# State-space stage of a transformer-like block: the residual as one more TensorE product of the output projection, rows copied out of PSUM by ScalarE

## What is computed

```python
def step(state, inp):                       # state [B, 512, 16]
    x_t, dt_t, B_t, C_t = inp
    dA = exp(clip(dt_t[:, :, None] * A[None], -10, 10))
    dB = dt_t[:, :, None] * B_t[:, None, :]
    state = clip(state * dA + x_t[:, :, None] * dB, -10, 10)
    y_t = einsum('bdn,bn->bd', state, C_t) + D * x_t
    return state, y_t
_, ys = lax.scan(step, state0, (x_in, dt, Bm, Cm))
y = ys * silu(z)
attn = y @ W_out                            # [.., 512] @ [512, 256]
x = x + attn + ffn(xn)                      # ffn: attention, shared expert, 2 of 7 routed experts
```

## Time and profile before

| | |
|---|---|
| median of 3 runs | 4429.94 us (4425.78 to 4437.9) |
| the profiled execution | 4428.19 us |
| its span, first to last instruction | 4426.1 us |
| mean granted TensorE clock | 0.930 of full speed |
| busy, whole span | TensorE 85%, VectorE 67%, ScalarE 57%, GpSimd 50% |
| addition of the residual, VectorE L1747 | 32 times, 682 ns each, at 2331.4 to 4422.8 us |

### The profile page before, as it was taken

One profiled execution on the slowest core, in us unless ns is written; L12 is line 12 of the kernel. 1 busy time (PEld: TensorE's weight loads), 2 busy tenths in 40 slices (PEclk: granted clock), 3 DMA queues, 4 the chain that ended last, 5 costly groups with the idle time before them and its releaser, 6 DMA issues.

```text
span 4426.1 us, 71771 instructions
## 1 busy us (share of the span) xinstructions
PE 3749.4 (85%) x22840; PEld 2837.4 (64%) x22840; DVE 2973.9 (67%) x5485; ACT 2502.8 (57%) x6473; POOL 2202.3 (50%) x1120
## 2 busy tenths in 40 slices
PE   4888888888888875999879888889998898888886
PEld 2444444444444434777658888878887888788776
DVE  4454444554545422222269999999999999999997
ACT  1443344334444341333278777788787787777773
POOL 2223333333333321000067777777777777777774
PEclk8899899999999987999989999999999999999998
DMA  2322232222322214666522222222222222222221
GB/s 85 96 82 83 79 95 82 84 79 93 97 88 85 81 51 117 212 213 208 161 89 92 76 87 78 80 87 87 75 92 85 78 92 76 87 80 78 87 82 36
DMA packets 285739, 419.89 MB, mean 95 GB/s; under 512 B 77397, under 2 KB 249814, under 8 KB 262808
## 3 DMA queue, kind: packets, MB, share of 16 engines
q1 hardware_dynamic: 273048, 381.12, 26.5%
q0 software_dynamic: 12288, 33.57, 2.2%
HBM read 330.63 MB, written 83.17 MB: 93 GB/s over the span
## 4 chain that ended last, share of the span: by engine, by line
POOL 22%; issue 10%; DVE 9%; PE 8%; ACT 1%; DVEq 0%; POOLq 0%; DMA 0%; SPq 0%; ACTq 0%
POOL m_ub L1516 18%; PE m_Y L1870 7%; DVE m_PR L1720 2%; DVE m_S L1728 2%; DVE m_PR L1728 2%; DVE m_S L1720 2%; POOL m_th_z L1501 1%; POOL m_yg L1526 1%; DVE m_ub L1705 1%; POOL m_dtx L1495 1%; ACT m_dA L1626 0%; PE m_F L1881 0%; PE m_F L1832 0%; PE m_F L1806 0%; DVEq L1719 0%
## 5 line engine op out<-in xcount | busy, mean ns | idle before, releaser
L1516 POOL TENSOR_TENSOR m_ub<-m_Bb,m_dtx 128x2048 f32<-128x2048 f32 x256 | 1157.5, 4544 | 436.3 <-PE m_Y L1870 429.9
L1626 ACT ACTIVATE m_dA<-m_dt,m_a_neg 128x128 f32<-128x128 f32 x4096 | 1211.1, 388 | 168.1 <-DVE m_S L1728 166.9
L1870 PE MATMUL m_Y<-m_ub,m_ident 128*128 128x128 f32 x8192 | 1040.9, 293 | 204.4 <-DVE m_ub L1705 204.4
L1870 PEld LDWEIGHTS m_Y<-m_ub,m_ident 128*128 128x128 f32 x8192 | 1022.7, 208 | 218.2 <-DVE m_ub L1705 218.2
L539 ACT ACTIVATE f_pt<-f_X 128x512 f32<-128x512 f32 (+1 forms) x704 | 372.2, 554 | 725.2 <-PE f_X L831 674.8
L615 DVE TENSOR_REDUCE f_nm<-f_Y 128x1 f32<-128x512 f32 (+3 forms) x896 | 434.1, 531 | 365.7 <-PE f_Y L825 339.6
L1720 DVE SCALAR_TENSOR_TENSOR m_PR<-m_dA,m_S 128x512 f32<-128x512 f32 x512 | 355.8, 695 | 123.1 <-POOL m_ub L1516 52.2
L824 PE MATMUL f_Y<-f_kst,f_qst 96*128 96x512 bf16 (+3 forms) x1024 | 281.9, 331 | 107.1 <-DVE f_nm L615 89.9
L1720 DVE SCALAR_TENSOR_TENSOR m_S<-m_dA,m_PR 128x512 f32<-128x512 f32 x512 | 355.1, 694 | 12.1
L1728 DVE CUSTOM_DVE_ANT_1 m_PR<-m_PR,m_ub 128x512 f32<-128x512 f32 x512 | 353.8, 691 | 0.2 <-DVE m_PR L1720 0.2
L1728 DVE CUSTOM_DVE_ANT_1 m_S<-m_S,m_ub 128x512 f32<-128x512 f32 x512 | 353.8, 691 | 0.0
(11 more groups left out here) (229 smaller groups left out, 6530.7 us busy)
## 6 DMA issues: line engine op xcount, KB each, us to landing
m_Bb<-m_bc_dram SPq DMA_DIRECT2D x64, 1024.0 KB, 4.5
m_Cb<-m_bc_dram SPq DMA_DIRECT2D x64, 1024.0 KB, 4.6
f_parts_dram<-f_parts SPq DMA_DIRECT2D x32, 768.0 KB, 4.1
f_kst<-f_parts_dram SPq DMA_DIRECT2D x192, 128.0 KB, 2.6
f_qst<-f_parts_dram SPq DMA_DIRECT2D x192, 128.0 KB, 2.6
e_rows<-sorted_rows SPq DMA_DIRECT2D x70, 256.0 KB, 2.7
e_wg<-Wg SPq DMA_DIRECT2D x70, 256.0 KB, 2.9
e_wu<-Wu SPq DMA_DIRECT2D x70, 256.0 KB, 3.9
```

The source lines that it names most:

```text
L1516: pool.tensor_tensor(ub[:, h, i, :, :], Bb[:, s, :, :], dtx[:, par, m, None, s * SN:(s + 1) * SN].to_broadcast([P, NST, SN]), ALU.mult).th ...
L1626: last = act.activation(dA[:, h, i, n, :], dtt[:, par, m, s * SN:(s + 1) * SN], ACT.Exp, scale=a_neg[:, m, n:n + 1])
L1870: last = pe.matmul(Y[:, i * SN:(i + 1) * SN], ident[:, :], ub[:, h, i, n, :], start=False, stop=(n == NST - 1), skip_group_check=True)
```

## The change

The addition leaves VectorE. In `project_out` each row block gets a seventh product, the identity times `res`, in the same accumulation, so `F[2]` holds the finished rows; TensorE now waits for `res_loaded`. ScalarE copies `F[2]` into `ot` (`copy_out`), behind `decays(c, par, 2)` and ahead of `softplus(c + 1)`, and signals `ot_done` as VectorE did.

```diff
@@ ScalarE @@
+        def copy_out(c):
+            act.wait_ge(outp_done, c + 1)
+            act.wait_ge(ot_stored, 16 * c)
+            act.activation(ot[:, :, :], F[2][:, :, :], ACT.Copy).then_inc(ot_done, 1)
...
             if not first:
                 decays(c, par, 2)
+                copy_out(c - 1)
...
-        chunk_order(body, lambda c, par: None)(nc.scalar)
+        def tail(c, par):
+            copy_out(c)
+        chunk_order(body, tail)(nc.scalar)
@@ VectorE @@
-        def add_res(c):
-            dve.wait_ge(outp_done, c + 1)
-            dve.wait_ge(res_loaded, 16 * (c + 1))
-            dve.wait_ge(ot_stored, 16 * c)
-            dve.tensor_tensor(ot[:, :, :], F[2][:, :, :], res[:, :, :], ALU.add).then_inc(ot_done, 1)
...
-                slots[1][1] = lambda: add_res(c - 1)
...
             gate_y(c, par, NU - 1)
-            add_res(c)
@@ TensorE, project_out @@
             pe.wait_ge(wdiag_ready, NY * (c + 1))
+            pe.wait_ge(res_loaded, 16 * (c + 1))
             pe.wait_ge(ot_done, c)
...
                 for k in range(TOPK):
-                    last = pe.matmul(F[2][:, j, :], wdiag[:, k, j, :], yg[:, k, j, :],
-                                     start=False, stop=(k == TOPK - 1))
+                    pe.matmul(F[2][:, j, :], wdiag[:, k, j, :], yg[:, k, j, :], start=False, stop=False)
+                last = pe.matmul(F[2][:, j, :], ident[:, :], res[:, j, :], start=False, stop=True)
             last.then_inc(outp_done, 1)
```

## The result

| | before | changed |
|---|---|---|
| median of 10 runs each | 4427.86 us | 4458.46 us |
| range | 4416.92 to 4438.88 | 4441.31 to 4487.55 |
| ratio, 95% interval | | 1.0073 (1.0050 to 1.0095) |
| profiled execution, its span | 4428.19, 4426.1 | 4448.95, 4447.2 |
| from the stage's first sum to the end of the span | 2167.4 | 2187.2 |

A forecast was written before the change was run, and what follows sets the result against it. Bound: the serial path from gating through projection, `dt_proj`, half a sum and GpSimd's two products to unit 2. Terms 25.8 - 0.6 + 0.86 - 0.1 = 26.0 us on the median 4429.94 gave 4455.9 us; range 4436 to 4472.

The forecast's parts named there:

- The bound: At unit 2, VectorE, though 95% busy, waits 0.90 us for GpSimd, so its removed addition gains nothing there.
- Two products, 0.86 us, on the path: In the projection, ahead of `dt_proj` and the sum of unit 0: two unhidden TensorE products cost 0.86 us a chunk.
- The idle time at unit 2: VectorE's wait before unit 2 grows from 0.90 to 2.35 us, and where it is 0.5, to about 2.0.
- The copy and the later `ot_done`: ScalarE's 0.6 us copy costs nothing; `ot_done` comes 5.5 us later, still 1.9 us ahead of `project_a`.
- VectorE's busy time: A sign in the new profile: VectorE's busy time falls by 32 x 0.68 = 22 us without a gain.
- The distance between copies: A sign: copies of successive chunks lie 68.3 us apart on average, where additions lay 67.46 apart.
- The sign: The forecast's check in the new profile that copies of successive chunks lie 68.3 us apart on average.
- The ends: Chunk 0 costs nothing; the last chunk gives back 0.6 us; the tail adds 0.86 and saves 0.1.
- The clock's mix, taken as unchanged: TensorE's mix of slow (8.88 us) and full-clock (7.31 us) sums stays; its ends, 17 us down and 20 up, guided the range.
- rival 2: More work keeps TensorE's clock up, winning back up to 17 us, to 4439 us, within the noise; chance 0.15.

The follow-up runs named there:

- e2: Changed kernel without the two residual products, so nothing adds the residual; ratio 0.9984 to the kernel before, median 9.2 us lower, stage 3.8 us longer.
- e3: Changed kernel with both residual products issued twice; 47.2 us over the kernel before, ratio 1.0093, stage 53.7 us longer.
- e1: Changed kernel with the copy to `ot` done by VectorE at the addition's old place, not by ScalarE; 15.8 us over the kernel before, ratio 1.0037.
- the second measurement: The changed kernel itself run again, nothing altered; 26.9 us over the kernel before, ratio 1.0049, stage 20.2 us longer.
- e6: Changed kernel with `dt_proj` issued behind the sum of unit 0 instead of ahead; 34.3 us over the kernel before, ratio 1.0068.
- e5: Kernel before, addition still on VectorE, with `dt_proj` issued behind the sum of unit 0; 27.6 us faster than the kernel before, ratio 0.9933.
- e11: e6 with ScalarE's `weigh` moved behind the copies for the convolution; 24.1 us faster than the kernel before, ratio 0.9945.
- the swap: On the changed kernel, `dt_proj` issued behind the sum of unit 0 instead of ahead, as in e6; 34.3 us over the kernel before.

## Why the prediction was right

It said 4455.9 us, +26.0, and the medians say 4458.46, +30.6, with an interval of 22 to 42 us. Step by step:

- *The bound.* That VectorE, busy for 95% of the loop, is not last at unit 2 was read from the 0.90 us of idle time there. e2 bears it out: with its addition taken away the stage is no shorter. VectorE's waits once per turn of the loop, which the prediction left out, don't bear on unit 2.
- *Two products, 0.86 us, on the path.* 0.86 in the timeline; in 24 chunks of the loop 0.84 and 0.75 a chunk in the two traces, and 0.90 for each two of e3's four, a price of 20 us or so for a predicted 20.6.
- *The idle time at unit 2.* Predicted 2.35 us and about 2.0; 2.41 in the row above, and 1.9 to 2.3 in every second chunk of the loop.
- *The copy and the later `ot_done`.* Predicted 1.9 us of margin ahead of `project_a`, measured 2.2. e1 against the changed kernel shows no price of it in the loop.
- *VectorE's busy time.* Predicted 22 us less, measured 16.6: the page counts overlapping instructions once, and the addition overlapped its neighbours. It took up 0.59 us from start to start, 18.9 us in 32 times; the last 2 were not traced.
- *The distance between copies.* Predicted 68.3 us, measured (4444.0 - 2338.8) / 31 = 67.9 (`m_ot` by tile, first and last copy). The sign was ill chosen: within a chunk the copy comes some 5.5 us later than the addition did, in the tail it does not. From VectorE's start of chunk 1 to that of chunk 31 the chunks lie 68.3 us apart, 67.6 before.
- *The ends.* This is the mis-sized term. The forecast has 4 x 0.86 - 0.6 + 0.86 - 0.1 = 3.6 us from the start of chunk 27 to the end. Measured, this part took 359.7 us before (4066.39 to 4426.1) and 358.1 and 358.2 in the two traces of the changed kernel: 1.6 us less, so 5 us of the 26 are missing here. TensorE spent 4.6 us less in the sums there too (174.8 against 179.4), so this may be the clock; e3, with 178.3 us in them, took 365.1, 5.4 more than before for four products. It was not tested, and stays open.
- *The clock's mix, taken as unchanged.* It did change: 26.6 us less were spent in the sums. But 20.9 of these lie in the 24 chunks, which paid nearly the full price all the same; TensorE waited more there instead, ahead of the sums above all (213.9 us over the whole trace, 204.4 before). By e3's price two products cost 21.5 us there, and the two traces have 20.2 and 18.1, so a gain of rival 2's kind is 1 to 3 us in the loop; whether the missing 5 us at the end are the clock's stays open. More work alone does not bring it, for e3, with still more of it, has the old sum again (1041.4). The pattern of slow and full-speed sums, which changed from pair to pair before, repeats from pair to pair through most of the changed kernel's trace; why was not tested. The Trainium skill, TensorE: Matmul & The Clock Gate, Part 1 (The HAM clock gate), says that activity releases the throttle; e3 shows no such release from activity added at this place.
- The medians exceed the stage's 20 us by 7 to 11. Execution times of one kernel spread over 17 to 55 us, and in part this arises ahead of the stage (17.8 us between the two traces of one kernel). The interval of the second measurement, 12 to 32 us, has the 20 in it; that of the first, 22 to 42, does not. Whether the unprofiled executions have another clock mix stays open. So the path and its price are shown, and that the medians came to lie within 5 us of the forecast is in part luck: the stage alone gives 6 us less than it.

## What to carry to other kernels

An engine that is busy for 95% of a loop need not be its bound: look at who arrives last at each hand-over, and a wait of 0.9 us there decides. Work moved from an engine that then waits onto the engine it waits for is a loss of its whole length; ahead of the event that the second engine is itself waiting for, the same work is nearly free. An edit that pays on one version of a pipeline can lose on its near twin, since every slack is a microsecond or two; after each move look again at which wait has grown.

## What was not expected

- Waits of 2.4 to 2.5 us on TensorE (e6) were followed by products at the lower clock in 28 of 29 chunks, those of 1.6 us at the same place (e5) in 6 of 12, those of 1.3 us (e11) in 5 of 29. So moving 1.26 us of ScalarE's work halved the wait and took away most of the slow stretches, 55 us in the stage over 30 chunks.
- A wait for GpSimd that is 0.90 us long was booked to VectorE's own last instruction, and one of 2.41 us under "issue". Only the ends of the other engines' instructions told what it was.
- With the swap, TensorE spent 958 us in the sums in place of 1041, all of them at the full clock in most chunks, and the kernel was slower than before all the same. Less time in the sums is no gain where they are not what arrives last.
